# An adaLN transformer block on one core: the prologue's work in another order, four modulations made as rows, and the last unit's VectorE, ScalarE, GpSimd and SyncE work in other places

## The reference

```python
mod = (silu(c) @ wmod).reshape(2, 6, 1, 512)
sa, ca, ga, sb, cb, gb = (mod[:, m] for m in range(6))   # both gates: kept away from zero, abs at least 0.25
h = layernorm(x) * (1 + ca) + sa
q, k, v = rope(h @ wq), rope(h @ wk), h @ wv   # 32 query heads, 8 key heads, HD = 128
att = softmax(causal(q @ k.T / sqrt(128)))
x = x + ga * ((att @ v) @ wo)
h = layernorm(x) * (1 + cb) + sb
x1, x2 = split(h @ w12.T + b12)
x = x + gb * ((silu(x1) * x2) @ w3.T + b3)
```

## Time and profile before

| what | value |
| --- | --- |
| median of 3 runs | 833.8 us |
| profiled execution | 831.21 us |
| its span, first to last instruction | 829.2 us |
| TensorE busy | 788.9 us (95%) |
| VectorE busy | 604.7 us (73%) |
| GpSimd busy | 568.5 us (69%) |
| ScalarE busy | 502.1 us (61%) |
| mean granted TensorE clock | 0.969 |

### The profile page before, as it was taken

How to read it: one execution, slowest core, us unless ns; L and a number is a source line. 1 busy time by engine, 2 the same in 40 slices (tenths; PEclk the granted TensorE clock), 3 DMA queues, 4 the chain that set the end, 5 groups by cost and what they waited for, 6 DMA issues and landing times.

```text
span 829.2 us, 11702 instructions
## 1 busy us (share of the span) xinstructions
PE 788.9 (95%) x3680; PEld 652.1 (79%) x3680; DVE 604.7 (73%) x1244; ACT 502.1 (61%) x1191; POOL 568.5 (69%) x384
## 2 busy tenths in 40 slices
PE   7879989989999999999999999999999998888997
PEld 2769868877888888888888888888888776766885
DVE  5866467867777877777778777878787778558785
ACT  2244576557667766776677667776677764864341
POOL 1464395768777887788777867797777996356453
PEclk9789799999999999999999999999999999999999
DMA  9612746577667756776677568866667855979011
GB/s 320 203 39 60 223 125 169 139 171 240 155 187 192 241 138 186 195 229 148 187 195 240 135 186 196 254 162 208 158 207 198 256 139 166 266 224 259 0 51 51
DMA packets 191885, 147.13 MB, mean 177 GB/s; under 512 B 62673, under 2 KB 168273, under 8 KB 189777
## 3 DMA queue, kind: packets, MB, share of 16 engines
...
...
## 4 chain that ended last, share of the span: by engine, by line
PE 57%; POOL 13%; ACT 8%; DVE 8%; DMA 7%; SPq 4%; issue 2%; DVEq 0%; ACTq 0%; POOLq 0%
PE out_bank L571 13%; PE q_bank L504 13%; PE s_bank L504 8%; PE o_bank L557 7%; PE x_bank L504 6%; POOL pT_lo L1344 5%; DMA spread_dram<-turned 5%; POOL wo_lo_sb L1344 3%; ACT probs L1139 3%; ACT probs L1147 2%; POOL rope_tmp L1370 2%; PE o_bank L512 2%; DVE turned L827 2%; POOL qT L1344 2%; SPq L339 2%
## 5 line engine op out<-in xcount | busy, mean ns | idle before, releaser
L1344 POOL TENSOR_TENSOR pT_lo<-pT_raw,pT_hi 128x1024 fp32r<-128x1024 f32 (+1 forms) x96 | 194.6, 2042 | 62.9 <-ACT pT_hi L1116 62.9
L1139 ACT ACTIVATE probs<-probs,neg_max 128x32 f32<-128x32 f32 (+15 forms) x256 | 130.6, 512 | 170.2 <-DVE neg_max L808 170.2
L1344 POOL TENSOR_TENSOR qT<-rope_tmp,qT 128x512 fp32r<-128x512 f32 x64 | 83.2, 1300 | 97.6 <-ACT qT L1116 97.6
L504 PE MATMUL s_bank<-kT,qT 128*128 128x32 f32 (+15 forms) x768 | 125.2, 312 | 8.3 <-POOL qT L1344 6.0
L827 DVE STREAM_TRANSPOSE turned<-probs 128x512 f32<-128x512 f32 (+1 forms) x64 | 96.7, 1511 | 44.9 <-DMA spread_dram<-turned 39.9
L504 PEld LDWEIGHTS s_bank<-kT,qT 128*128 128x128 f32 x768 | 115.4, 193 | 17.7 <-issue 4.9
L1370 POOL TENSOR_TENSOR rope_tmp<-rope_tmp 128x512 f32<-128x512 f32 x80 | 109.3, 1374 | 27.1 <-DVE rope_tmp L785 27.1
L1147 ACT ACTIVATE probs<-probs,row_inv 128x32 f32<-128x32 f32 (+15 forms) x256 | 111.9, 508 | 0.7 <-DVE row_inv L817 0.7
L808 DVE CUSTOM_DVE_ANT_0 probs<-s_bank,mask_sb 128x32 f32<-128x32 f32 (+15 forms) x256 | 98.5, 433 | 17.9 <-PE s_bank L504 17.7
L571 PE MATMUL out_bank<-wo_hi_sb,attn_hi 128*128 128x512 f32 x248 | 100.0, 403 | 12.0 <-POOL wo_lo_sb L1344 6.6
L504 PE MATMUL q_bank<-hT_hi,wq_hi_sb 128*128 128x512 f32 x248 | 101.3, 408 | 2.7 <-DVE rope_tmp L785 2.5
...
## 6 DMA issues: line engine op xcount, KB each, us to landing
...
```

The lines of the kernel that those rows point to most:

```text
L504: last = pe.matmul(dst, lhs(a, cc), rhs(b, cc), start=(k == 0), stop=(k == len(todo) - 1))
L1139: nc.scalar.activation(rows, rows, ACT.Exp, bias=neg_max[:, par, t:t + 1], scale=-1.0, accum_out=row_sum[:, par, t:t + 1]).then_inc(exp_do ...
L1344: nc.gpsimd.tensor_tensor(dst, src, hi.bitcast(f32), ALU.subtract).then_inc(done, 1)
```

## The change

The prologue: modulations 3, 5, 4 and 2 are made by `modulation_rows`, in that order, into a bank that is free at the place, copied by ScalarE (`copy_rows`) and turned by `turn_rows`; `modulation` is gone. Modulation 3 moves ahead of the third query head and waits for a bank alone, 5 and 4 stand in slot 1, 2 in slot 2. All four query heads of batch 0 now come before v, and the first projection of batch 1 comes behind the first scores, into out_bank in place of q_bank. ScalarE normalises the second batch, which VectorE did, and copies modulations 0 and 1 out of PSUM; VectorE works out the second batch's scale before the low parts of the first, and does its low parts of h behind the fifth rotation, the sixth in slot 0. GpSimd splits all of the first weights ahead of the rotations.

The last unit: the statistics, the maxima of slots 4 and 7, the exponents of slot 5, the inverses and the joins stand in other places, and the w12 loads leave the places ahead of the last two writes of turned blocks.

The diff, cut to its core and without the eight leading blanks that all its lines share; in the order mod tables, SyncE, TensorE, VectorE, ScalarE, GpSimd:

```diff
-mod_row = [rope_tmp[0:B, 0, m, :] for m in range(2)]
-mod_banks = [q_bank, out_bank]
+MODS = [0, 1, 3, 5, 4, 2]
+mod_banks = [q_bank, out_bank, out_bank, x_bank, x_bank, out_bank]
+mod_row = [rope_tmp[0:B, 0, 0, :], rope_tmp[0:B, 0, 1, :], f_blocks[0:B, :], f_raw[0:B, :], f_raw[0:B, :], f_blocks[0:B, :]]
...
-rope_banks = [x_bank, q_bank, out_bank, q_bank, out_bank, q_bank]
+rope_banks = [x_bank, q_bank, out_bank, q_bank, out_bank, out_bank]
...
-    load_wq(0, 1)
+    for h in range(1, REP):
+        load_wq(0, h)
+    load_wv(0)
     load_wmod(3)
-    load_wq(0, 2)
-    load_wv(0)
-    load_wq(0, 3)
...
-            if s >= 4 and last:
+            if s in (4, 5) and last:
                 load_w12(s - TT)
+            if s == 5 and last:
+                load_w12(2)
...
     blocks_to_keys(KV - 1, SLOTS - 1)
+    load_w12(3)
...
-        for n in range(KC):
-            at = 2 * (KC * m + n)
-            for k in range(KC):
-                last = pe.matmul(o_bank[:, at:at + 2], wmod_blocks[m][:, k, n * P:(n + 1) * P],
-                                 c_silu[:, :, k], start=(k == 0), stop=(k == KC - 1))
-        last.then_inc(mod_made, 1)
...
             r = s % TT
             scores(g, s)
+            if first and s == 0:
+                pe.wait_ge(roped, 5)
+                project_q(out_bank[:, :], 1, 0, h_lo[1])
             if first and s == 1:
-                modulation(4)
+                pe.wait_ge(roped, ROPE_FIRST)
+                modulation_rows(5)
             if first and s == 2:
-                modulation(5)
-                modulation(2)
+                turn_rows(5)
+                turn_rows(4)
+                modulation_rows(2)
...
+            if first and s == 1:
+                pe.wait_ge(roped, ROPE_FIRST + rope_k_at(0) + 1)
+                modulation_rows(4)
+            if first and s == 2:
+                turn_rows(2)
...
-                project_k(batch_of(v), h_lo[1] if first and s == 0 else None)
+                project_k(batch_of(v))
...
-    def modulation_rows(m, part):
-        pe.wait_ge((wmod_half_in, wmod_in)[part][m], 16)
-        for k in range(part * KC // 2, (part + 1) * KC // 2):
-            last = pe.matmul(mod_banks[m][0:B, :], c_silu[:, :, k], wmod_blocks[m][:, k, :],
-                             start=(k == 0), stop=(k == KC - 1))
-        if part == 1:
+    def modulation_rows(m, part=None):
+        for k in range(KC):
+            if part in (None, k * 2 // KC):
+                if k == 0 and part == 0:
+                    pe.wait_ge(wmod_half_in[m], 16)
+                elif part is None or k == KC // 2:
+                    pe.wait_ge(wmod_in[m], 16)
+                last = pe.matmul(mod_banks[m][0:B, :], c_silu[:, :, k], wmod_blocks[m][:, k, :],
+                                 start=(k == 0), stop=(k == KC - 1))
+        if part != 0:
             last.then_inc(mod_rows, 1)
     def turn_rows(m):
-        pe.wait_ge(mod_rows_copied, m + 1)
+        pe.wait_ge(mod_rows_copied, MODS.index(m) + 1)
...
     modulation_rows(0, 1)
     modulation_rows(1, 0)
     pe.wait_ge(ident_in, 16)
-    pe.wait_ge(x_normed, TT)
...
     project_q(q_bank[:, :], 0, 0)
     pe.wait_ge(wq_lo, 2)
     project_q(out_bank[:, :], 0, 1)
-    pe.wait_ge(mod_ready, 1)
-    modulation(3)
+    pe.wait_ge(x_normed[1], TT)
+    turn_x(1, range(KC))
+    pe.wait_ge(roped, 1)
+    modulation_rows(3)
     pe.wait_ge(roped, 2)
     pe.wait_ge(wq_lo, 3)
     project_q(q_bank[:, :], 0, 2)
-    pe.wait_ge(x_normed, B * TT)
-    turn_x(1, range(KC))
-    pe.wait_ge(wv_lo, 1)
-    project_v(0)
     pe.wait_ge(roped, 3)
     pe.wait_ge(wq_lo, 4)
     project_q(out_bank[:, :], 0, 3)
-    pe.wait_ge(roped, 4)
-    project_q(q_bank[:, :], 1, 0, h_lo[1])
+    pe.wait_ge(mod_ready, 2)
+    turn_rows(3)
+    pe.wait_ge(wv_lo, 1)
+    project_v(0)
...
+            if last and s == 3:
+                x1_stats(0)
             invert(g, s)
+            if first and s == 0:
+                turn_blocks(g, s)
+                first_rotation(ROPE_FIRST - 1)
             if last and s == 3:
+                x1_stats(1)
                 x1_stats(2)
                 add_x1(3)
                 attn_low(g, 0)
...
-            if last and s == 2:
-                x1_stats(0)
-                x1_stats(1)
...
     def last_unit():
         g = KV - 1
+        maxima(g, 4)
         norm_scale(0, B + 1)
-        maxima(g, 4)
         attn_low(g, 1)
+        add_out(g, 0)
         invert(g, 4)
         turn_blocks(g, 4)
-        add_out(g, 0)
         attn_low(g, 2)
         maxima(g, 5)
-        invert(g, 5)
         for k in range(KC):
             h2_low(0, k)
+        invert(g, 5)
...
         maxima(g, 6)
         add_out(g, 2)
         invert(g, 6)
+        maxima(g, 7)
         turn_blocks(g, 6)
-        maxima(g, 7)
         invert(g, 7)
...
     dve.wait_ge(x_in[2], 16)
     for w in range(TT, 2 * TT):
         nc.vector.bn_stats(stats[:, w, :], acc[:, w, :]).then_inc(stats_made, 1)
-    dve.wait_ge(mod_made, 2)
-    link(nc.vector.tensor_copy(mod[:, 0:2 * KC, :].rearrange("p m b -> p (m b)"), o_bank[:, 0:4 * KC]))
-    nc.vector.tensor_scalar(one_plus[:, 0:KC, :], mod[:, KC:2 * KC, :], 1.0, None, ALU.add).then_inc(mod_ready, 1)
+    norm_scale(1, 2)
...
-    first_rotation(0)
-    norm_scale(1, 2)
-    first_rotation(1)
-    norm_x(1)
-    first_rotation(2)
-    first_rotation(3)
+    for n in range(ROPE_FIRST - 1):
+        first_rotation(n)
     for k in range(KC):
         h_low(k)
-    first_rotation(4)
     dve.wait_ge(h_lo[1], KC)
     turn_v(0, 1)
     for par in range(2):
         for n in range(1, QT):
             nc.vector.memset(probs[par][:, PLACES[par] - 1, n, 0:n, :], 0.0)
-    first_rotation(5)
...
+            if last and s == 3:
+                q_high(g, s - 1)
             exponents(g, s)
-            q_high(g, s - 1)
+            if first and s == 0:
+                normalise(g, s)
+            if not (last and s == 3):
+                q_high(g, s - 1)
             if r == 1:
                 k_high(g, s - 1)
             v = (SLOTS * g + s) // TT
             if r == 0 and (s > 0 or not first) and (v == 1 or fresh(v - 1)):
                 for n in range(REP):
                     wo_high(LOAD[v - 1], n)
-            normalise(g, s)
+            if last and s == 3:
+                attn_high(g, 0)
+            if first and s == 1:
+                copy_rows(5)
+            if not (first and s == 0):
+                normalise(g, s)
+            if first and s in (1, 2):
+                copy_rows((4, 2)[s - 1])
             if first and s == 3:
                 act.wait_ge(mod_made, 6)
-            if last and s == 3:
-                attn_high(g, 0)
...
         probs_high(g, 2)
+        attn_high(g, 1)
         norm_x1(0)
-        attn_high(g, 1)
         exponents(g, 4)
         normalise(g, 4)
         attn_high(g, 2)
         modulate_x1(0, (0, 1))
-        exponents(g, 5)
         modulate_x1(0, (2, 3))
         probs_high(g, 3)
+        exponents(g, 5)
         normalise(g, 5)
...
-        act.wait_ge(mod_rows, m + 1)
+        act.wait_ge(mod_rows, MODS.index(m) + 1)
+        if m in (4, 2):
+            act.wait_ge(mod_made, MODS.index(m) - 1)
...
-    act.wait_ge(mod_ready, 1)
+    act.wait_ge(mod_made, 2)
+    nc.scalar.activation(mod[:, 0:2 * KC, :].rearrange("p m b -> p (m b)"), o_bank[:, 0:4 * KC],
+                         ACT.Copy).then_inc(mod_ready, 1)
+    nc.scalar.activation(one_plus[:, 0:KC, :].rearrange("p m b -> p (m b)"), o_bank[:, 2 * KC:4 * KC],
+                         ACT.Copy, bias=1.0).then_inc(mod_ready, 1)
+    act.wait_ge(mod_ready, 2)
     for k in range(KC):
         modulate_x(0, k)
     wq_high(0, 1)
+    act.wait_ge(norm_ready, 2)
+    for w in range(TT, 2 * TT):
+        nc.scalar.activation(acc[:, w, :], acc[:, w, :], ACT.Identity, bias=shift[:, w, :],
+                             scale=rstd[:, w, :]).then_inc(x_normed[1], 1)
     wq_high(0, 2)
+    wq_high(0, 3)
+    wv_high(0)
     rotated_high(0, 0, kT[0][0][:, :])
     rotated_high(0, 1, qT[0][0][:, :, 0, :])
-    wv_high(0)
-    wq_high(0, 3)
+    modulate_x(1, 0)
+    modulate_x(1, 1)
     rotated_high(0, 2, qT[0][0][:, :, 1, :])
-    for k in range(KC):
-        modulate_x(1, k)
+    copy_rows(3)
+    modulate_x(1, 2)
+    modulate_x(1, 3)
...
-            if g == KV - 2 and s == 7:
-                join_x(0)
-            if last and s >= 1:
-                join_x(s)
             q_low(g, s - 1)
             if r == 1:
                 k_low(g, s - 1)
+            if g == KV - 2 and s == 7:
+                join_x(0)
+            if last and s in (1, 2):
+                join_x(s)
...
+            if last and s == 2:
+                join_x(3)
...
-    wq_low(0, 0)
-    wq_low(0, 1)
+    for h in range(REP):
+        wq_low(0, h)
+    wv_low(0)
     rotated_sum(0, 0)
-    wq_low(0, 2)
     rotated_low(0, 0, kT[0][0][:, :], kT[1][0][:, :])
-    rotated_sum(0, 1)
```

(9 more changed lines are left out.)

20 lines of the change are left out of this document (10 added, 10 removed).

## The result

The changed kernel takes 821.2 us (median of 4, 819.49 to 823.52) against 833.7 before (median of 4, 832.64 to 834.23). The ratio is 0.9856, 95% interval 0.9833 to 0.9879: some 12.0 us less, 10.1 to 13.9. The forecast was 824.4, with 819.5 to 829.0 around it.

The account below looks back on a forecast made before the run. TensorE bounds the middle, so gains lie in the first 100 us and the last unit. Start 15.0 - 10.6 = 4.4, last unit 5.0: 9.4 us off 833.8 gives 824.4, range 819.5 to 829.0.

Parts of the forecast that it names:

- case A: Whole kernel: start and last unit gain as summed, 9.4 us; 824.4, own range 821.5 to 827; chance 0.58.
- (a): Start: modulations with c as weights and 512 moving columns cost nothing more, at worst 0.6 us for all four.
- (b): Start: four times four small transposes, 0.40 us each time, add 1.6 us.
- (c): Start: VectorE's second-batch scale ahead of the first cast delays the first k projection, 1.2 us; 0.1 to 3.0.
- (d): Start: the wait before the first scores, for the fourth query head's low part, shrinks from 4.5 to 2.7 us.
- (e): Start: new wait of slot 0's query for the sixth rotation, 3.1 us, bounds 2.1 and 3.1.
- case B: Start gives little: both projections behind the new waits run at 1.2 GHz, 5.3 instead of 2.0; 827.7; chance 0.13.
- (f): Last unit: GpSimd's q low part ahead of the join removes the 1.4 wait; smaller waits shrink; 2.0 us upstream.
- (g): Last unit: w12 loads moved from ahead of SyncE's last two writes of turned blocks gain 1.6 + 2.0 = 3.6 us.
- (h): Last unit: maxima of slots 4 and 7 moved earlier; their waits (2.3, 2.4) lie beside the blocks' chain; no gain added.
- Case C: Last unit gives little: ScalarE's late slot 5 exponents keep its turning from coming earlier; 827.8; chance 0.11.
- E: First unit: products with two weight columns do not keep the clock up; 11.3 us slower, 845.1; chance 0.03.

Follow-up runs that it names:

- before_again: The kernel before the change, unchanged, executed once more for a second trace: 836.2 us (one execution).
- blocks_back: Changed kernel with modulations 5, 4 and 2 made by blocks again, without their copies and turnings: 828.4 us, ratio 0.9922.
- after: The changed kernel as first measured, against the kernel before the change: 821.2 us, ratio 0.9856.
- act_old: Changed kernel with slot 5's exponents back at their old place on ScalarE, ahead of modulation and slot 3's split: 819.3 us, ratio 0.9811.
- dve_old: Changed kernel with VectorE's order of the last unit as before: 828.4 us, ratio 0.9921.
- join_old: Changed kernel with GpSimd's joins ahead of q's low part in the last unit, as before: 821.4 us, ratio 0.9841.
- start_only: Changed kernel with all edits of the last unit taken back on all four engines: 828.1 us, ratio 0.9910.

## Why the prediction was right, and where it was not

The direction and the range held; the gain came out larger than forecast, 12.0 against 9.4, so that 821.2 lies just under the 821.5 to 827 of case A. Part of the agreement is luck: the terms below miss by up to 2.8 us, in both directions, and one of the prediction's own signs of being wrong came true. Step by step:

**Removed at the start: 15.0, and more.** The wait and the low clock of the third query projection, the low stretch of 7.8 and the low clock of modulations 5 and 2 went as computed. The step that fell short is "modulations 5 and 2 at the full clock ... 2.6" and its neighbour 2.1: sized from one execution, which was a good one. In before_again they are 11.43 - 7.3 = 4.1 and 5.23 - 3.03 = 2.2, and the projection behind modulation 4, which stood at 1.00 in the trace I had, adds 1.3. blocks_back shows that it is the form of the matmuls that brings the low clock down on what follows. The sentence that rows "kept 1.00 earlier" was the right row to read.

**(a), (b), (c).** A modulation took 3.60, as taken. The sets of turnings took 0.3 to 0.4 each on TensorE. The scale of the second batch cost little: one link beside GpSimd took 1.21 and the first k projection began at 22.64 against 22.10, 0.5 late in this pair of traces where I took 1.2.

**(d)** The wait is 3.6 where I took 2.7, at my upper side: the sum took 1.71 and the low part 1.53 beside VectorE's low parts of h. By the Trainium skill (SBUF — State Buffer, Who interferes with whom) each of the two could have waited for up to a whole VectorE instruction, which I had put at 0.7; the trace shows 0.4 and 0.2 on GpSimd, so the rule has the direction, and my estimate by it was about twice the size.

**(e)** 2.2 in place of 3.1. My reason, that VectorE would come 1 us late, was wrong: it stood waiting for TensorE, since batch 1's query ran at a low clock and ended only at 58.4; the rotation began at 58.45.

**The clock behind the two waits: 2.0 taken, 4.3 measured.** Scores 2.63 against 1.56, the query behind them 4.71 against 3.03, slot 0's query 4.50 against 3.03: 1.1 + 1.7 + 1.5 = 4.3. That is nearer to case B's 5.3 than to my 2.0; "less than half, as both waits are shorter than 4.5" was no reason. Waits of 3.6 and 2.2 brought the clock down in after as 4.5 did before: low over most of both projections, the sign by which I had said the prediction would be wrong. Of the other traces with the wait of 2.2 two, act_old and dve_old, kept 1.00 behind it (3.03 and 3.02 for slot 0's query). Sum of what was added: 1.4 + 0.5 + 3.6 + 2.2 + 4.3 = 12.0, so 15.0 - 12.0 = 3.0, and slot 3 of the first unit did come 95.40 - 92.20 = 3.2 earlier in this pair of traces. Against the usual old start it is 5.3. So two errors of opposite sign, 2.8 and more on what was removed and 1.4 on what was added, left the 4.4 near the truth: rival B's mechanism came, at 2.3 of its 3.3 us, and did not decide.

**"Whatever is gained ahead of it moves everything behind by the same amount."** True over all traces (5.3 at slot 3 and 5.3 at group 2, as means), but not in a pair: of the 3.2 only 1.2 were left at group 2. Each execution has low stretches of its own there: from 110 to 130 us the clock was 1.00 before and 0.91 after, from 180 to 200 us 0.91 before and 1.00 after.

**(f)** Its size was there, its mechanism not. From group 7's first scores to those of its slot 4 the old order needed 44.7, 44.9 and 43.2 us, the new one 41.2 (mean of seven): 3.0 less, where I took 2.0. But it is 41.2 in join_old too, so the join's place is worth nothing there, and 41.2 in dve_old, so it is not VectorE's order by itself. What gives it stays open; ScalarE's high parts ahead of slot 3's exponents were taken back in no run but start_only, with all the rest. **(g)** was right, 3.0 against 3.6. One thing I had not seen: the writes' own issue is slower behind the loads. **(h)** was set to nothing with the words "TensorE can follow it, no more". The distance from slot 4's to slot 5's scores fell from 11.3 to 9.4 or 9.5 in the traces with the whole new order (10.0 in join_old), and was 12.2 in dve_old. But this 1.8 did not last: from slot 5's to slot 7's scores the new order needs 25.2 against 23.2, 2.0 more, as much as the new wait for maxima before slot 7's scores. So nothing was near the truth as a sum, though not because TensorE only follows the chain. By place, the 6.9 of the last unit are 3.0 up to slot 4's scores, 1.8 to slot 5's, -2.0 to slot 7's and 4.0 behind them; of the last, 3.0 are shown to be the loads. What gives the other 3.9 stays open: dve_old, which was to tell, mixed VectorE's order with ScalarE's.

**Case C** (late exponents of slot 5 take the gain back) did not happen; **E** is out: the modulations made as rows ran at full clock in every trace.
